# Gates of a top-2 expert layer carried in the scattered rows and applied where a tile's results leave PSUM

## The chip, the cores and the metric

The kernel runs on one NeuronCore of one Trainium2 chip. The metric is the device time of one launch in microseconds (us). TensorE (PE), VectorE (DVE), ScalarE (ACT), GpSimd (POOL) and SyncE (SP) each follow their own instruction stream; they meet only through semaphores. SP issues most DMAs, POOL the indirect ones that scatter rows.

## The reference, cut to what matters

Input `x` is 64 x 64 x 16 x 16 (f32). Two quantised 3x3 convolutions with batch norms form the first half, and a mixture of 8 experts with two choices for each of the 16384 tokens forms the second.

```python
x = x + conv_ref(ln_over_channels(x), ...)       # two BN + 4-bit act + 3x3 conv layers, plus residual
t = to_tokens(x)                                  # 16384 tokens x 64 channels
flat = layernorm(t)
logits = flat @ router_w.T                        # 8 experts
probs = softmax(logits)
topk_probs, topk_idx = top_k(probs, 2)
topk_probs = topk_probs / (sum(topk_probs, -1, keepdims=True) + 1e-09)
gates = einsum('nk,nke->ne', topk_probs, one_hot(topk_idx, 8))
h = silu(flat @ w1[e].T) * (flat @ w3[e].T)       # hidden size 682
y = h @ w2[e].T
t = t + einsum('ne,nec->nc', gates, y)            # only the two chosen experts count
x = from_tokens(t)
```

## The kernel before, in words

**Stages.** The image data lies as 16 stripes of 512 pixels by two halves of 64 channels, and stripes are worked in 8 pairs. First come the channel norm and the first convolution (to about 96 us of the span). Then follows the *route* stage (about 96 to 209 us): for each pair of stripes `route(p)` on each engine does the second convolution, the token norm, the router's logits, the choice of two experts and the slot of each token in a table of rows by expert, `expert_rows` in DRAM. A row holds 64 channels, the token's number and the preference code of its first choice (`ROW = C + 2`, line 43). Beside it the weights of one expert per pair are turned and written to DRAM (`stack_weights` on PE, line 1302, `w_stacked` copies on ACT, lines 685 to 690). Then a map of tiles is made on DVE (to about 218 us).

**Route on DVE** (line 950) is a chain of small instructions, each waiting for the one before. Work of the next pair is put between them: `add_conv` (line 942) for pair p+1, which needs that pair's convolution from PE, and the rounding of pair p+2. After `chosen` (line 994) PE makes the positions (lines 1323 to 1326) and the logits of pair p+1, and then the convolution of pair p+2 (line 1273). DVE takes the positions up at line 1002 and ends the pair with the slots (line 1008). The logits less their maximum stay in `lg` for all pairs, and the second choice's in `top2`.

**Route on ACT** (line 673) takes a square root of 16 numbers per row (line 675), two scaled copies for the rounding (649), four copies of the turned weights (685 to 690), two copies of the new x (668) and two squares (671). Exp of all pairs runs once after the last pair (lines 701 and 702), then Silu's table is fetched (703).

**Tiles.** 68 tiles of 512 rows (the last 12 are made of two halves with different experts) run through `tile` on every engine. SP loads rows and weights; PE turns the rows (1360), multiplies up (1387, both halves of the array), and down (1402), and turns the results back (1368); ACT does Silu (709 to 713) and the PSUM copies (720, 727); DVE multiplies (`hidden`, 1126 and 1130), copies the turned results to rows (`rows_out`, 1142) and prepares the tile after next (`split`, 1111 to 1117: which choice a row is, its target row, and a rearranged copy). POOL scatters 128 rows per instruction, in an order fixed when the program is built (lines 567 to 573): 256 scatters of token rows (551) and 270 of result rows (561). Result rows go to `result_rows` in DRAM, first choices in the lower half, second choices in the upper.

**Final stage.** When all scatters have landed, SP loads the results back as 8 pairs for each choice (486), named `y_and_rows` (first choice) and `conv_all` (second). For each pair ACT multiplies the first choice by its gate in 16 pieces (748), POOL the second choice in one instruction (581), DVE adds the two (1190), PE turns the sum (1430), DVE adds it to x (1185), and SP stores (494). SP issues no store before it has issued all loads. The gates themselves are computed on DVE from the exponentials (lines 1172 to 1178) while the last scatters run.

## Time and profile before

| what | value |
|---|---|
| median of 3 runs | 852.25 us (847.7 to 852.38) |
| profiled execution | 846.57 us, span 844.6 us, mean TensorE clock 0.929 |
| PE / PEld busy | 749.0 (89%) / 430.8 us (51%) |
| DVE / ACT / POOL busy | 553.6 (66%) / 491.9 (58%) / 557.2 us (66%) |
| route, 99 to 209 us | eight pairs, 11.3 to 14.7 us each |
| tiles, 226 to 792 us | 68 tiles, 8.26 us each |
| final stage, 800 to 844.6 us | loads, gates, sums, stores |

The span is cut into busy time by engine on the page; the idle time before an instruction and what ended it stand in brackets in a timeline. PE's clock is given as the share of full speed: 1.00 is 2.4 GHz and 0.50 is 1.2 GHz. POOL's busy time leaves out the 0.30 us between two of its scatters, so 66% does not mean a third of it is free.

### The profile page before, as it was taken

The page shows a single profiled execution, that of the slowest core. Times are in us where ns is not written, and L with a number is a line of the kernel's source. Part 1 is how long each engine was busy: PE and PEld are TensorE (multiplying, and loading weights), DVE is VectorE, ACT ScalarE, POOL GpSimd, SP SyncE. Part 2 cuts the span into 40 slices and gives each one's busy share as a digit, 9 for nine tenths or more (in the row PEclk, how much of TensorE's full clock was granted, in tenths as well). Part 3 has the DMA queues.
Part 4 walks back from the last instruction along what each step waited for, and adds up shares of the span by engine and source line. Part 5 has one row for each costly group of instructions (what it writes and reads, how often), then busy time and mean ns, then how long its engine had stood idle before and what let it go on. Part 6 is the DMA issues. An engine that isn't in the chain of part 4 may idle for free.

```text
span 844.6 us, 17550 instructions
## 1 busy us (share of the span) xinstructions
PE 749.0 (89%) x4875; PEld 430.8 (51%) x4875; DVE 553.6 (66%) x1326; ACT 491.9 (58%) x1127; POOL 557.2 (66%) x572
## 2 busy tenths in 40 slices
PE   5959688985499999999999999999999999999534
PEld 3734266664154555545454554545454557777323
DVE  5977578788466565666666565666676666666455
ACT  5836444333266666666666666666666566666285
POOL 3520027777777777777777777777777777777561
PEclk9959889897599999999999999999999999999855
DMA  8760023343344434343343434343334356656096
GB/s 199 133 111 0 0 62 102 112 135 108 103 120 122 127 108 126 110 117 113 112 113 112 121 104 127 114 112 113 112 113 111 113 158 180 191 168 181 26 387 195
DMA packets 84226, 104.98 MB, mean 124 GB/s; under 512 B 27061, under 2 KB 57966, under 8 KB 84176
## 3 DMA queue, kind: packets, MB, share of 16 engines
q1 hardware_dynamic: 65040, 83.17, 34.8%
q0 software_dynamic: 19136, 21.28, 9.3%
q14 instruction: 35, 0.29, 0.1%
q8 instruction: 15, 0.25, 0.1%
HBM read 73.62 MB, written 27.02 MB: 119 GB/s over the span
## 4 chain that ended last, share of the span: by engine, by line
PE 79%; DVE 9%; ACT 5%; issue 4%; DMA 1%; POOL 1%; DVEq 0%; SPq 0%; ACTq 0%; POOLq 0%
PE bank L1387 40%; PE bank L1402 21%; PE bank L1273 7%; ACT y_and_rows L748 4%; PE bank L1368 3%; PE bank L1360 2%; PE bank L1213 2%; PE bank L1218 1%; PE bank L1287 1%; PE bank L1294 1%; PE bank L1229 1%; DVE stats L972 1%; DMA conv_all<-result_rows 1%; DVE y_and_rows L959 0%; DMA w<-expert_w 0%
## 5 line engine op out<-in xcount | busy, mean ns | idle before, releaser
L551 POOL DMA_INDIRECT expert_rows<-y_and_rows,slot_all x256 | 249.4, 974 | 143.8 <-issue 77.2
L1126 DVE TENSOR_TENSOR conv_all<-conv_all,bank 128x512 f32<-128x512 f32 x340 | 233.7, 687 | 165.1 <-ACT conv_all L709 163.6
L1387 PE MATMUL bank<-xT,w 64*128 64x512 f32 (+1 forms) x1608 | 326.4, 536 | 1.8 <-DMA w<-expert_w 1.7
L709 ACT ACTIVATE conv_all<-bank 128x512 f32<-128x512 f32 x340 | 203.0, 597 | 118.3 <-PE bank L1387 118.0
L1387 PEld LDWEIGHTS bank<-xT,w 64*128 64x128 f32 x1608 | 144.9, 187 | 172.1 <-DVE conv_all L1126 85.4
L561 POOL DMA_INDIRECT result_rows<-conv_all,dest_all x142 | 140.1, 986 | 46.7 <-issue 41.8
L1402 PE MATMUL bank<-conv_all,w 128*64 128x256 f32 x1240 | 161.7, 384 | 1.2 <-DVE tile_map L1098 1.2
L1402 PEld LDWEIGHTS bank<-conv_all,w 128*64 128x64 f32 x1240 | 91.1, 136 | 51.6 <-issue 12.6
L720 ACT ACTIVATE xT<-bank 64x256 f32<-64x256 f32 x272 | 102.8, 378 | 14.1 <-PE bank L1360 11.7
L1273 PE MATMUL bank<-quant_padded,conv_w_blocks 128*128 128x512 bf16 x288 | 73.8, 418 | 8.7 <-issue 4.4
L727 ACT ACTIVATE conv_all<-bank 128x256 f32<-128x256 f32 x68 | 26.0, 383 | 86.0 <-PE bank L1402 86.0
L561 POOL DMA_INDIRECT result_rows<-result_rows,dest_all x64 | 63.2, 987 | 19.5 <-issue 19.2
L561 POOL DMA_INDIRECT result_rows<-squares,dest_all x64 | 63.0, 985 | 19.5 <-issue 19.2
L1273 PEld LDWEIGHTS bank<-quant_padded,conv_w_blocks 128*128 128x128 bf16 x288 | 29.7, 106 | 49.2 <-issue 15.4
L1130 DVE TENSOR_TENSOR rstd_wide<-conv_all,bank 42x256 f32<-42x256 f32 x136 | 52.0, 422 | 2.1
L1430 PE MATMUL bank<-ident,y_and_rows 128*128 128x128 f32 x64 | 15.7, 427 | 30.9 <-DVE y_and_rows L1190 30.9
L1402 PE MATMUL bank<-rstd_wide,w 128*64 128x256 f32 x248 | 40.9, 379 | 0.0
L748 ACT ACTIVATE y_and_rows<-y_and_rows,gates 128x64 f32<-128x64 f32 x128 | 30.7, 337 | 13.2 <-DMA conv_all<-result_rows 13.2
L1360 PE MATMUL bank<-ident,conv_all 128*128 128x128 f32 x136 | 26.3, 276 | 5.1 <-DVE conv_all L1117 5.1
L1368 PE MATMUL bank<-ident,conv_all 128*128 128x128 f32 x136 | 29.8, 301 | 0.5 <-ACT conv_all L727 0.5
L1430 PEld LDWEIGHTS bank<-ident,y_and_rows 128*128 128x128 f32 x64 | 12.6, 224 | 34.0 <-DVE y_and_rows L1190 34.0
L530 POOL DMA_DIRECT2D x_all<-y_and_rows x16 | 15.9, 1173 | 20.4 <-DVE y_and_rows L849 20.4
(248 smaller groups left out, 844.7 us busy)
## 6 DMA issues: line engine op xcount, KB each, us to landing
w<-expert_w SPq DMA_DIRECT2D x68, 384.0 KB
w<-expert_w SPq DMA_DIRECT2D x68, 192.0 KB
conv_all<-expert_rows SPq DMA_DIRECT2D x56, 132.0 KB
x_all<-in_x SPq DMA_DIRECT2D x16, 256.0 KB, 4.1
x_all<-y_and_rows POOLq DMA_DIRECT2D x16, 256.0 KB, 4.8
expert_rows<-y_and_rows,slot_all POOLq DMA_INDIRECT x256
y_and_rows<-result_rows SPq DMA_DIRECT2D x8, 512.0 KB, 9.8
conv_all<-result_rows SPq DMA_DIRECT2D x8, 512.0 KB, 10.6
```

The source lines that it names most:

```text
L551: nc.gpsimd.indirect_dma_start(xs, bass.IndirectOffsetOnAxis(ap=slot_all[:, s, k * GH + g:k * GH + g + 1], axis=0), rows_all[:, s, g, :], ...
L561: nc.gpsimd.indirect_dma_start(yout, bass.IndirectOffsetOnAxis(ap=dest_all[:, j, g:g + 1], axis=0), yrow[j % RING][:, g, :], None, bounds_ ...
L709: nc.scalar.activation(sbuf[k % 3], h1_ps[k % 3][:], ACT.Silu).then_inc(silu_rdy, 1)
L720: ins = nc.scalar.activation(xT[u][C * h:C * h + C, TH * t:TH * t + TH], turn_ps[C * t:C * t + C, 0:TH], ACT.Copy)
L748: ins = nc.scalar.activation(y[:, g, :], y[:, g, :], ACT.Copy, scale=gate[:, 0, 2 * p + g // GH, g % GH:g % GH + 1])
L1126: V.tensor_tensor(hbuf[k], sbuf[k % 3], h3_ps[k % 3][:], ALU.mult).then_inc(mul_rdy, 1)
L1130: ins = V.tensor_tensor(hbuf[k][0:HR, rows_], sbuf[k % 3][0:HR, rows_], ps[k % 3][TAIL3:TAIL3 + HR, rows_], ALU.mult)
L1273: ins = mm(conv_ps[u][:], wblk[:, l, t, :], qpad[u][:, :, ky:ky + H, kx:kx + W], start=t == 0, stop=t == TAPS - 1)
L1360: ins = nc.tensor.transpose(turn_ps[:, 128 * q:128 * q + 128], pairs_x[u][:, q, :], ident[:])
L1368: ins = nc.tensor.transpose(turn_ps[:, TH + 128 * q:TH + 128 * q + 128], ysb[u][:, 128 * q:128 * q + 128], ident[:])
L1387: ins = mm(ps[k % 3][:, rows_], w[half, cols], xT[u][half, rows_], start=True, stop=True)
L1402: ins = mm(y_ps[C * e:C * e + C, 0:TH], w2buf[e * two][u][:, i, :], hbuf[i][:, TH * e:TH * e + TH], start=i == 0, stop=i == KT - 1)
```

## The change

The row gets two more numbers (`ROW = C + 4`): the gate of the first choice, and what must be added to it to get the gate of the second. They are computed in every pair of the route stage, by `gates` on DVE (five instructions) from exponentials that ACT now makes pair by pair (`exps`). Sqrt and Exp lie in different activation tables, so ACT switches the table twice in each pair, each time by a dummy activation placed ahead (`load_table`). In a tile, `split` picks the gate of each row (two more instructions of 4 numbers each), and `rows_out` multiplies by it instead of copying. The final stage has only the sum on DVE; the multiplications on ACT (128 instructions) and on POOL (8) and the seven gate instructions on DVE are gone.

```diff
-    ROW = C + 2
+    ROW = C + 4
@@ POOL, end
-            pool.wait_ge(gate_rdy, 1)
-            for p in range(NP):
-                pool.wait_ge(yk_in[p], 32)
-                y = yk[1][p].rearrange("p (g c) -> p g c", g=GP)
-                nc.gpsimd.tensor_tensor(y, y, gate_of(1, p), ALU.mult).then_inc(g2_rdy, 1)
@@ ACT, route
+            def load_table(f):
+                k = (ACT.Sqrt, ACT.Exp, ACT.Silu).index(f)
+                nc.scalar.activation(table_first[:, k:k + 1], half_col[:, 0:1], f)
+            def exps(p):
+                act.wait_ge(ex_go, p + 1)
+                nc.scalar.activation(lg[:], lg[:], ACT.Exp)
+                nc.scalar.activation(top2[:], top2[:], ACT.Exp).then_inc(ex_rdy, 1)
             def route(p, first=False, last=0):
                 act.wait_ge(rsd_rdy, 2 * p + 1)
                 nc.scalar.activation(st[:, 1, :], st[:, 0, :], ACT.Sqrt).then_inc(rsd_rdy, 1)
+                load_table(ACT.Exp)
...
+                if first:
+                    exps(p)
+                if last != 1:
+                    keep_x1(p + 1)
+                if not first:
+                    exps(p)
                 if last != 1:
                     squares(p + 1)
+                    load_table(ACT.Sqrt)
@@ ACT, end
-            act.wait_ge(gate_rdy, 1)
-            for p in range(NP):
-                act.wait_ge(yk_in[p], 32)
-                y = yk[0][p].rearrange("p (g c) -> p g c", g=GP)
-                for g in range(GP):
-                    ins = nc.scalar.activation(y[:, g, :], y[:, g, :], ACT.Copy,
-                                               scale=gate[:, 0, 2 * p + g // GH, g % GH:g % GH + 1])
-                ins.then_inc(g0_rdy, 1)
@@ DVE, route
+            def gates(p, c, rows_p):
+                total, below = gsum[:, 0], gsum[:, 1]
+                first_gate, change = rows_p[:, :, C + 2], rows_p[:, :, C + 3]
+                dve.wait_ge(ex_rdy, p + 1)
+                c(V.tensor_reduce(total, lg[:], AX.X, ALU.add))
+                c(V.scalar_tensor_tensor(below, total, 1e-9, top2[:], ALU.mult, ALU.add))
+                c(V.tensor_scalar(below, below, 1.0, None, ALU.add))
+                c(V.reciprocal(first_gate, below))
+                V.scalar_tensor_tensor(change, top2[:], -1.0, first_gate, ALU.add, ALU.mult)
...
+                gates(p, c, rows_p)
                 dve.wait_ge(pos_rdy, p + 1)
@@ DVE, split
                     ins = V.tensor_scalar(second[u][:, n * i:n * i + n], xrow[u][:, n * i:n * i + n, C + 1],
-                                          expert_of[:, two, at], float(TOK), ALU.not_equal, ALU.mult)
+                                          expert_of[:, two, at], None, ALU.not_equal)
                 c(ins)
-                V.tensor_tensor(dest_all[:, j, :], second[u][:], xrow[u][:, :, C], ALU.add)
+                c(V.tensor_tensor(gate_change[u], second[u], xrow[u][:, :, C + 3], ALU.mult),
+                  lambda: V.scalar_tensor_tensor(dest_all[:, j, :], second[u], float(TOK), xrow[u][:, :, C],
+                                                 ALU.mult, ALU.add))
+                V.tensor_tensor(gate_of_row[j % 4], gate_change[u], xrow[u][:, :, C + 2], ALU.add)
@@ DVE, rows_out
-                V.tensor_copy(yrow[r].rearrange("p (t q) c -> p q t c", t=2),
-                              turn_ps[:, TH:T].rearrange("p (q t c) -> p q t c", q=2, t=2)).then_inc(yr_sb, 1)
+                V.tensor_tensor(yrow[r].rearrange("p (t q) c -> p q t c", t=2),
+                                turn_ps[:, TH:T].rearrange("p (q t c) -> p q t c", q=2, t=2),
+                                gate_of_row[v].rearrange("p (t q) -> p q t", t=2).unsqueeze(3)
+                                .broadcast_to([128, 2, 2, C]), ALU.mult).then_inc(yr_sb, 1)
@@ DVE, end
-            dve.wait_ge(ex_rdy, 2)
-            one(V.tensor_reduce(gsum[:], lg[:], AX.X, ALU.add))
...
             for p in range(NP):
-                dve.wait_ge(g2_rdy, p + 1)
-                dve.wait_ge(g0_rdy, p + 1)
+                dve.wait_ge(yk_in[p], 32)
                 V.tensor_tensor(yk[0][p], yk[0][p], yk[1][p], ALU.add).then_inc(g1_rdy, 1)
```

How the instructions move, at three places. First VectorE in the last pair of the route stage, from `chosen` to the slots, before (the pairs of the loop have the same order with the two rounding instructions of line 911 behind the first row):

```order
L994 TENSOR_TENSOR chosen<-one_hot 128x128
L1002 TENSOR_TENSOR positions<-bank,base 128x136
L1004 TENSOR_TENSOR route_slots<-one_hot,positions 128x256
L1005 COPY base<-positions 128x8
L1006 COPY base_by_stripe<-positions 128x16
```

and in the changed kernel, where `gate_sum` is `gsum` and `y_and_rows` the token rows:

```order
L998 TENSOR_TENSOR chosen<-one_hot 128x128
L948 TENSOR_REDUCE gate_sum<-logits 128x16
L949 SCALAR_TENSOR_TENSOR gate_sum<-gate_sum,second_minus_first 128x16
L950 TENSOR_SCALAR gate_sum<-gate_sum 128x16
L951 RECIPROCAL y_and_rows<-gate_sum 128x16
L952 SCALAR_TENSOR_TENSOR y_and_rows<-second_minus_first,y_and_rows 128x16
L1007 TENSOR_TENSOR positions<-bank,base 128x136
L1009 TENSOR_TENSOR route_slots<-one_hot,positions 128x256
```

Five instructions now stand between `chosen` and the positions. Second, ScalarE from the last weight copy of the seventh pair (the one behind the loop) into the eighth, before:

```order
L690 ACTIVATE w_stacked<-bank 42x64
L668 ACTIVATE x_all<-x_0 128x512
L668 ACTIVATE x_all<-x_1 128x512
L671 ACTIVATE squares<-bank 128x512 x2
L675 ACTIVATE stats<-stats 128x16
```

and now:

```order
L690 ACTIVATE w_stacked<-bank 42x64
L660 ACTIVATE x_all<-x_0 128x512
L660 ACTIVATE x_all<-x_1 128x512
L669 ACTIVATE logits<-logits 128x128
L670 ACTIVATE second_minus_first<-second_minus_first 128x16
L665 ACTIVATE squares<-bank 128x512 x2
L654 ACT_TABLE_LOAD
L654 ACTIVATE table_first<-half_col 128x1
L674 ACTIVATE stats<-stats 128x16
L654 ACT_TABLE_LOAD
L654 ACTIVATE table_first<-half_col 128x1
```

The two exponentials stand ahead of the squares, one table load behind the squares and one behind the square root. Third, VectorE at the end of one of the last tiles, before:

```order
L1142 COPY squares<-bank 128x2x2x64
L1111 TENSOR_SCALAR conv_all<-conv_all,tile_expert 128x2 x2
L1114 TENSOR_TENSOR dest_all<-conv_all 128x4
L1117 COPY conv_all<-conv_all 128x256
L1126 TENSOR_TENSOR conv_all<-conv_all,bank 128x512 x5
```

and now:

```order
L1149 TENSOR_TENSOR conv_all<-bank,conv_all 128x2x2x64
L1115 TENSOR_SCALAR conv_all<-conv_all,tile_expert 128x2 x2
L1118 TENSOR_TENSOR conv_all<-conv_all 128x4
L1119 SCALAR_TENSOR_TENSOR dest_all<-conv_all 128x4
L1121 TENSOR_TENSOR conv_all<-conv_all 128x4
L1124 COPY conv_all<-conv_all 128x256
L1133 TENSOR_TENSOR conv_all<-conv_all,bank 128x512 x5
```

Two small instructions come in, and the copy of the results has become a product with the gate.

## Rows read from the trace of the kernel before

**Rows 1.** The page: chain that ended last, by engine.

```profile
PE 79%; DVE 9%; ACT 5%; issue 4%; DMA 1%; POOL 1%; DVEq 0%; SPq 0%; ACTq 0%; POOLq 0%
```

**Rows 2.** Windows: start:end, length, busy us (instructions) of each engine, clock, DMA share, GB/s.

```profile
226.00:607.00 381.00, 381.00 (x2388) 192.24 (x2389) 240.97 (x520) 243.88 (x551) 290.43 (x298) 0.99 0.41 117
692.00:792.00 100.00, 99.52 (x867) 73.40 (x863) 63.35 (x140) 62.67 (x141) 73.69 (x76) 1.00 0.56 163
```

**Rows 3.** Timeline, DVE, end of a tile: start, us, instruction, [idle before <-releaser].

```profile
408.24 0.42 DVE L1142 COPY conv_all<-bank 128x256 f32<-128x256 f32 x1 [0.50 <-ACT xT L720]
408.83 0.21 DVE L1114 TENSOR_TENSOR dest_all<-conv_all 128x4 int32<-128x4 f32 x1
411.08 0.69 DVE L1126 TENSOR_TENSOR conv_all<-conv_all,bank 128x512 f32<-128x512 f32 x1 [1.83 <-ACT conv_all L709]
```

**Rows 4.** Timeline, DVE, the sixth pair of the route stage.

```profile
177.55 0.25 DVE L825 RECIPROCAL stats<-stats 128x16 f32<-128x16 f32 x1 [0.28 <-ACT stats L675]
177.84 0.18 DVE L826 SCALAR_TENSOR_TENSOR stats<-stats 128x16 f32<-128x16 f32 x1
180.93 0.69 DVE L942 SCALAR_TENSOR_TENSOR x<-bank,x_all 128x512 f32<-128x512 f32 x1 [0.16 <-issue]
183.19 0.28 DVE L988 TENSOR_REDUCE second_minus_first<-route_a 128x128 f32 x1
186.16 0.30 DVE L1002 TENSOR_TENSOR positions<-bank,base 128x136 f32<-128x136 f32 x1 [0.19 <-PE bank L1326]
```

**Rows 5.** Timeline, DVE, its longer waits in other pairs of the route stage.

```profile
128.90 0.69 DVE L942 SCALAR_TENSOR_TENSOR x<-bank,x_all 128x512 f32<-128x512 f32 x1 [1.22 <-PE bank L1273]
130.93 0.69 DVE L942 SCALAR_TENSOR_TENSOR x<-bank,x_all 128x512 f32<-128x512 f32 x1 [1.14 <-PE bank L1273]
157.25 0.69 DVE L942 SCALAR_TENSOR_TENSOR x<-bank,x_all 128x512 f32<-128x512 f32 x1 [1.46 <-PE bank L1273]
197.47 0.30 DVE L1002 TENSOR_TENSOR positions<-bank,base 128x136 f32<-128x136 f32 x1 [0.87 <-issue]
207.98 0.30 DVE L1002 TENSOR_TENSOR positions<-bank,base 128x136 f32<-128x136 f32 x1 [1.32 <-issue]
```

**Rows 6.** Timeline, PE: the convolution of a pair at either clock.

```profile
150.61 6.34 PE L1273 MATMUL bank<-quant_padded,conv_w_blocks 128*128 128x512 bf16 x18
163.31 4.21 PE L1273 MATMUL bank<-quant_padded,conv_w_blocks 128*128 128x512 bf16 x18
```

**Rows 7.** Windows inside those two convolutions (columns as in Rows 2).

```profile
150.00:155.00 5.00, 5.00 (x15) 2.19 (x16) 4.28 (x14) 1.71 (x3) 3.78 (x5) 0.50 0.09 27
163.50:167.50 4.00, 4.00 (x20) 1.82 (x19) 3.35 (x10) 1.71 (x3) 3.01 (x4) 1.00 0.54 194
```

**Rows 8.** Timeline, ACT: the second pair, the sixth pair, and the two late table loads.

```profile
124.22 0.22 ACT L675 ACTIVATE stats<-stats 128x16 f32<-128x16 f32 x1 [1.50 <-DVE stats L973]
...
181.82 0.87 ACT L685 ACTIVATE w_stacked<-bank 128x512 f32<-128x512 f32 x2 [2.81 <-PE bank L1310]
184.90 1.10 ACT L671 ACTIVATE squares<-bank 128x512 f32<-128x512 f32 x2
...
210.83 1.28 ACT L703 ACT_TABLE_LOAD   x1
212.12 0.20 ACT L703 ACTIVATE silu_first<-half_col 128x1 f32<-128x1 f32 x1
```

**Rows 9.** Timeline, final stage: the three multiplying and adding engines.

```profile
805.08 30.66 ACT L748 ACTIVATE y_and_rows<-y_and_rows,gates 128x64 f32<-128x64 f32 x128 [13.16 <-DMA conv_all<-result_rows]
...
825.02 2.35 POOL L581 TENSOR_TENSOR conv_all<-conv_all,gates 128x1024 f32<-128x1024 f32 x1 [1.12 <-DMA conv_all<-result_rows]
...
835.84 1.23 DVE L1190 TENSOR_TENSOR y_and_rows<-y_and_rows,conv_all 128x1024 f32<-128x1024 f32 x1 [1.40 <-ACT y_and_rows L748]
```

**Rows 10.** Windows of the final stage (columns as in Rows 2).

```profile
802.00:825.00 23.00, 7.87 (x32) 6.28 (x32) 11.63 (x11) 19.92 (x84) 14.23 (x7) 0.50 1.04 386
839.50:844.10 4.60, 0.00 (x0) 0.00 (x0) 0.32 (x1) 0.00 (x0) 0.00 (x0) 0.50 0.83 228
```

More of the change, by code:

```diff
@@ L147, in conv_moe_kernel @@
         counts = bases[:, SNAPS[0] - 1:NS, :]
-        gate = sb("gates", [128, 2, NS, GH])
-        gsum = sb("gate_sum", [128, NS, GH])
         tm = sb("tile_map_work", [128, 8, LV, E])
@@ L192, in conv_moe_kernel @@
         second = [carve(4) for u in range(2)]
+        gate_change = [carve(4) for u in range(2)]
+        gate_of_row = [carve(4) for v in range(4)]
         ysb = [carve(TH) for u in range(2)]
@@ L359, in conv_moe_kernel @@
         fin_ps = [bank[0:2], bank[2:4]]
-        def gate_of(k, p):
-            return gate[:, k, 2 * p:2 * p + 2, :].rearrange("p a g -> p (a g)").unsqueeze(2).broadcast_to([128, GP, C])
         NSMALL = 2 + 1 + 1
@@ L668, in squares @@
                     nc.scalar.activation(stripe(xb, s), x1[u][:], ACT.Copy).then_inc(x1_kept, 1)
+            def squares(p):
                 for u in range(2):
@@ L691, in route @@
                                      ACT.Copy).then_inc(wt_sb, 1)
+                if first:
[4 more added lines that the diff above has]
+                    exps(p)
                 if last != 1:
                     squares(p + 1)
+                    load_table(ACT.Sqrt)
             for s in range(4):
                 affine(1, s, s % 2)
+            keep_x1(0)
             squares(0)
             pairs(act, route)
-            act.wait_ge(ex_go, 1)
-            nc.scalar.activation(lg[:], lg[:], ACT.Exp).then_inc(ex_rdy, 1)
-            nc.scalar.activation(top2[:], top2[:], ACT.Exp).then_inc(ex_rdy, 1)
-            nc.scalar.activation(silu_first[:], half_col[:, 0:1], ACT.Silu)
+            load_table(ACT.Silu)
             def silu(j, k):
@@ L1167, in _ @@
             rows_out(NT - 1, 3, (NT - 1) % RING)
-            g0, g1 = gate[:, 0], gate[:, 1]
-            dve.wait_ge(ex_rdy, 2)
-            one(V.tensor_reduce(gsum[:], lg[:], AX.X, ALU.add))
-            one(V.reciprocal(g0, gsum[:]))
-            one(V.tensor_tensor(g1, top2[:], g0, ALU.mult))
-            one(V.scalar_tensor_tensor(gsum[:], g0, 1e-9, g1, ALU.add, ALU.add))
-            one(V.reciprocal(gsum[:], gsum[:]))
-            for k in range(2):
-                ins = V.tensor_tensor(gate[:, k], gate[:, k], gsum[:], ALU.mult)
-            ins.then_inc(gate_rdy, 1)
             def add(p):
```

21 lines of the change are left out of this document (9 added, 12 removed).

## The prediction

> **What bounds the kernel now.** I read the chain of waits by engine first: PE holds 79% of it [rows 1]. Then the stages in windows. In the tile stage PE is busy 381.0 of 381 us and 99.5 of 100 [rows 2]; 68 tiles at 8.26 us. POOL has nearly no air either: 298 instructions with 0.30 us behind each are 290.4 + 89.4 = 379.8 us of 381, and in the second window 73.7 + 76 x 0.30 = 96.5 of 100 [rows 2]. DVE and ACT have a third of their time free there. Then a timeline of one tile: DVE ends its work behind a tile and waits 1.83 us for ACT's Silu of the next [rows 3]. In the route stage DVE is the bound of the pairs in which PE's clock is full: in the sixth pair the only waits over 0.2 us are for the square root, and DVE comes to `add_conv` with the convolution done, 0.16 us of issue [rows 4]. Where the clock is at half, DVE waits for the convolution, 1.22 and 1.14 us in the second pair and 1.46 in the fourth [rows 5]. Last the final stage: ACT's 128 multiplications run without a break for 30.66 us, while POOL, with 2.35 us per pair, waits for each load; the last pair's load is in by 825.02, its sum starts only at 835.84 [rows 9]. So ACT sets the end there, 10.8 us behind the data.
>
> **Final stage: a gain.** Removed: 128 ACT and 8 POOL instructions. The next limits are three.
> - The chain behind the last load. From the start of the last sum to the end of the span are 844.6 - 835.84 = 8.76 us [rows 9]. With the sum starting at 825.02 the end is 833.8, a gain of 10.8.
> - DVE itself: a sum of 1.23 us [rows 9] and two additions of 0.69 us (an addition from PSUM of this shape costs that, like 0.69 in [rows 4]) are 2.6 us per pair. Eight loads come between 805.1 and 825.0 [rows 9], 2.8 us apart. DVE just keeps up.
> - The DMA engines. They are full (share 1.04) at 386 GB/s from 802 to 825 [rows 10], 23 x 386 = 8.88 MB. The loads are 16 of 512 KB, 8.39 MB; so 0.49 MB of the 4.19 MB of stores is out by 825, and 3.70 MB are left. The stores no longer trickle behind ACT, they stand in a queue, so their rate decides. Upper end: 386 GB/s, 9.6 us, end 834.6. Lower end: the last four stores of before ran alone at 228 GB/s [rows 10]: 16.2 us, end 841.2. That row had a share of 0.83, so with a full queue it is 228 / 0.83 = 275 GB/s. As some stores will be mixed with loads I take 300: 12.3 us, 837.3. To that 0.5 us for the last landing (DMA is active to 844.1 in [rows 10], the span ends at 844.6).
>
> So the final stage ends near 837.8: **6.8 us gained**, between 2.9 and 9.5. The gate arithmetic that goes from DVE there ran beside the last scatters and is worth nothing.
>
> **Route stage: a loss on DVE.** `gates` adds a reduction of 128 numbers (0.28), three small instructions of 16 (0.18 each) and a reciprocal (0.25) [rows 4]. That is 1.07 us, with about 0.03 us of semaphore between each 1.2 us a pair. What covers it, pair by pair:
> - First pair: nothing, the next `add_conv` comes behind it in order. 1.2.
> - Second: the third pair has no wait for the convolution. 1.2.
> - Third: the fourth waits 1.46 us for its convolution [rows 5]. 0.
> - Fourth, fifth, sixth: only the 0.19 us wait for the positions [rows 4]. 3 x 1.0.
> - Seventh: 0.87 us before the positions [rows 5]. 0.3.
> - Eighth: 1.32 us before the positions, PE at half clock [rows 5]. 0.
>
> The waits of the second pair cover nothing, since its convolution is itself behind the first pair's delay. Sum **5.7 us**. If the waits covered all but the first two, 2.4; if none did, 9.6.
>
> **Route stage: ACT.** Per pair two table loads of 1.28 us with dummies of 0.20 [rows 8], and two exponentials of 128 and 16 numbers at 0.2 to 0.3 (the small activations of [rows 8] take 0.20 and 0.22): together 3.5 us. There is room: after the square root ACT waits 2.81 us for the weights, of which load and dummy take 1.5 [rows 8]. Tightest behind the squares is the second pair, with 1.50 us of idle before its square root [rows 8] against 1.48. The exponentials come behind the copies of x: in the sixth pair those end where the squares began, 184.90 [rows 8], so the exponentials end at 185.5, and DVE asks for them at 186.0, just before the old start of line 1002 [rows 4]. 0.5 us of margin. I cost ACT at nothing; if the cover goes, each late microsecond is one on DVE.
>
> The row shows that a table load costs its 1.28 us and no more: the next activation starts 0.01 us behind it [rows 8]. The Trainium skill (ScalarE: Activation LUTs, What ACT_TABLE_LOAD costs, and Table sets) puts a switch at 1283 ns and a drain of about 1380 ns more, and says to do all activations of one set before the next, which is just what this change gives up. By its 2.66 us, as an estimate, 14 more switches are 37 us of ACT; the second pair's square root would come some 1.4 us late and the rest would stay within the waits, so the sum would be about 1.5 us higher. The trace has the 1283 and not the drain.
>
> **Tile stage.** `split` gains two instructions of 4 numbers, 0.21 each [rows 3]. `rows_out` reads PSUM and multiplies instead of copying 256 columns, 0.42 [rows 3]; a product of twice the columns is 0.69 [rows 3], so the product lies between 0.42 and 0.69. At most 0.7 us more against 1.83 idle: hidden, in all tiles but two: the first, where the split is on the way to the first matmul (0.3), and the one in which DVE also places the half tiles, where its idle time is already used up (0.4). **0.7 us.**
>
> **POOL and the queues.** Token rows grow from 264 to 272 bytes. POOL's time is per instruction; if it went with the bytes instead, 3% of 256 x 0.97 is 7.5 us, and POOL has 3.5 us free in [rows 2] plus the later start of the tiles, 5.7 - 1.2 = 4.5, in which it runs ahead. So even then it is barely not the bound. I cost it at 0.
>
> **Sum.** 5.7 + 0.7 - 6.8 = -0.4: from 846.57 to 846.2 us. The profiled execution lay 5.7 us below the median of the runs shown and within them, so in their terms **852.0 us** (852.25 - 0.4, rounded).
>
> **The rivals.**
> - *The gain comes through and the route's loss does not* (13%). Half clock strikes the convolution in a few pairs, 6.34 us against 4.21 [rows 6], at clock 0.50 against 1.00 [rows 7]. PE works the same in a longer pair; should the drops fall elsewhere, in waits, the stage loses 1.5 instead of 5.7. With the final stage at the limit of its chain: 1.5 + 0.7 - 10.8 = -8.6, 843.7 against 852.25. For it: only three pairs are struck now. Against it: DVE's five instructions have no cover.
> - *PE's clock takes the route stage* (13%, slower). DVE's longer pair leaves PE waiting longer, and PE may drop to half clock in every pair. A convolution at half throughout is 2 x 4.21 = 8.4 us. In the fourth pair 6.34 us gave a wait of 1.46 [rows 5, 6]; with 8.4, and DVE 1.2 later, the wait is 1.46 + 2.1 - 1.2 = 2.4, in each of five pairs, 12 us, on top of the gates. It decides once a convolution passes 6.1 us. 852.0 + 12 = 864.
> - *ACT comes late* (4%, slower). If exponentials miss their 0.5 us margin, or Sqrt waits for its table, both loads of each pair enter DVE's chain: 8 x 1.3 to 8 x 2.6, 862 at the least. Against it: the idle times above.
> - *The product in `rows_out` or the wait for the gates delays the tiles*: needs 1.8 us per tile, which no row near it has (1%).
> - *DMA stores at 228 GB/s*: within my own case, +3.9.
>
> My forecast has 69%. **Range**: down, the final stage at 9.5 and a route of 2.4 (-6.4) and the lower runs of the same kernel (847.7, 4.5 below the median), partly together: 843. Up, 9.6 of route and 2.9 of gain (+7.4), and a part of the clock case: 861. A measurement here can tell about 1% from no change. Faster by over 1% (below 843.7) 0.13; within 0.69; slower 0.18.
>
> **What would show it.** Sums at line 1187 starting about 2.8 us apart, right behind the loads, the last near 825 plus the shift; DMA full between 802 and 838. In the route stage, pairs one, two, four, five and six 1 to 1.2 us longer, the third not; the start of the first tile at 226 + 6. Sixteen table loads of 1.28 us there, and no wait of line 948 for ACT. Tiles at 8.26 us as before. I am wrong if the convolution rows show half clock in more than three pairs, if the stores alone run nearer 228 or 386 GB/s, or if a DVE wait for ACT appears at line 948.

## The result, and the profile after

The changed kernel takes 846.36 us (median of 20 runs) against 849.91 us (20 runs of the kernel before on the same chip). The ratio is 0.9959, with a 95% interval of 0.9941 to 0.9978; in a later set of runs, on a chip of its own, the same kernel gave 0.9961 [0.9931, 0.9991]. So it is faster by 0.4%, within the 1% called no change above. The profiled execution went from 846.57 us (span 844.6) to 845.35 us (span 843.3, mean TensorE clock 0.925): -1.2 us where -0.4 was forecast. One further run of the changed kernel took 3324 us, once in 32, with no profile of it; the ratio leaves it out, and I have no cause for it.

By stages of the two profiled executions, each from the first instruction of its kind to that of the next stage:

| stage | before, us | after, us | measured | predicted |
|---|---|---|---|---|
| norm and first convolution, to the first rounding on DVE | 100.23 | 101.06 | +0.83 | 0 |
| route, to the map of tiles | 116.38 | 121.98 | +5.60 | +5.7 |
| map to first tile | 9.11 | 9.22 | +0.11 | 0 |
| tiles and last scatters | 574.42 | 575.40 | +0.98 | +0.7 |
| final, from the first load's issue | 44.46 | 35.64 | -8.82 | -6.8 |
| sum | 844.60 | 843.30 | -1.30 | -0.4 |

The chain of waits by engine answers to [rows 1]: ACT's share has fallen from 5% to 2%, DVE's has risen from 9% to 12%.

```profile
PE 75%; DVE 12%; issue 5%; DMA 2%; ACT 2%; SPq 2%; POOL 1%; DVEq 1%; POOLq 0%; ACTq 0%
```

The windows of the changed kernel, columns as in [rows 2]. The first two lie in the tile stage, moved by the 6 to 8 us by which it starts later; the others in the final stage and answer to [rows 10].

```profile
232.00:613.00 381.00, 380.74 (x2376) 191.84 (x2378) 249.86 (x608) 243.44 (x551) 290.00 (x297) 0.99 0.41 117
700.00:800.00 100.00, 99.44 (x864) 73.35 (x864) 64.76 (x158) 62.68 (x141) 70.69 (x72) 1.00 0.55 162
810.00:830.00 20.00, 11.81 (x48) 9.41 (x48) 14.35 (x17) 0.00 (x0) 0.00 (x0) 0.50 1.05 390
830.00:834.00 4.00, 3.04 (x13) 2.64 (x14) 3.75 (x6) 0.00 (x0) 0.00 (x0) 0.50 1.08 383
834.00:838.00 4.00, 0.90 (x5) 0.50 (x3) 1.45 (x3) 0.00 (x0) 0.00 (x0) 0.50 1.09 383
838.00:842.00 4.00, 0.00 (x0) 0.00 (x0) 0.00 (x0) 0.00 (x0) 0.00 (x0) 0.50 1.04 357
```

PE is as full in the tile stage as before. In the final stage the DMA engines are full from 810 us to the last store: the stores that ran with nothing beside them moved 383 and then 357 GB/s, not the 300 of the forecast. That rate is one of the prediction's own signs of being wrong ("nearer 228 or 386 GB/s"). The timeline of DVE there:

```profile
812.72 1.23 DVE L1187 TENSOR_TENSOR y_and_rows<-y_and_rows,conv_all 128x1024 f32<-128x1024 f32 x1 [12.33 <-DMA conv_all<-result_rows]
815.43 1.23 DVE L1187 TENSOR_TENSOR y_and_rows<-y_and_rows,conv_all 128x1024 f32<-128x1024 f32 x1 [1.49 <-DMA conv_all<-result_rows]
816.57 1.28 DVE L1183 TENSOR_TENSOR x_all<-x_all,bank 128x512 f32<-128x512 f32 x2
...
831.65 1.22 DVE L1187 TENSOR_TENSOR y_and_rows<-y_and_rows,conv_all 128x1024 f32<-128x1024 f32 x1 [0.26 <-DMA conv_all<-result_rows]
```

Eight sums, 2.71 us apart, each released by its load; the last starts at 831.65, 11.6 us before the end, where in [rows 9] it started 8.8 us before it. What follows the last sum is longer now (stores still queue), but it starts with the data.

The route stage. First VectorE in the fifth pair, from `chosen` to the next pair's reduction:

```profile
176.14 0.29 DVE L998 TENSOR_TENSOR chosen<-one_hot 128x128 bf16<-128x128 f32 x1
176.34 0.76 DVE L905 TENSOR_SCALAR quant_padded<-quant_tmp 128x512 bf16<-128x512 f32 x2
177.01 0.28 DVE L948 TENSOR_REDUCE gate_sum<-logits 128x16 f32<-128x128 f32 x1
177.33 0.17 DVE L949 SCALAR_TENSOR_TENSOR gate_sum<-gate_sum,second_minus_first 128x16 f32<-128x16 f32 x1
177.53 0.25 DVE L950 TENSOR_SCALAR gate_sum<-gate_sum 128x16 f32<-128x16 f32 x1
177.92 0.26 DVE L951 RECIPROCAL y_and_rows<-gate_sum 128x16 f32 x1
178.32 0.19 DVE L952 SCALAR_TENSOR_TENSOR y_and_rows<-second_minus_first,y_and_rows 128x16 f32 x1
178.43 0.29 DVE L1007 TENSOR_TENSOR positions<-bank,base 128x136 f32<-128x136 f32 x1
...
180.33 1.22 DVE L976 TENSOR_REDUCE stats<-squares 128x16 f32<-128x1024 f32 x1 [0.33 <-issue]
```

From the first of the five gate instructions (177.01) to the positions (178.43) are 1.42 us, with no wait for ACT and none for the matmuls of the positions, for which DVE waited 0.19 us before [rows 4]. In the fourth and the sixth pair (windows of 13.77 and 13.45 us) some instructions that stand in every pair take longer, here in the fourth the two roundings, 0.93 us where the fifth has 0.76:

```profile
162.70 0.93 DVE L905 TENSOR_SCALAR quant_padded<-quant_tmp 128x512 bf16<-128x512 f32 x2
```

Next PE and DVE in the second pair:

```profile
121.80 3.76 PE L1284 MATMUL bank<-centre_half,x 128*128 128x128 f32 x16 [3.72 <-DVE x L936]
126.22 1.22 DVE L976 TENSOR_REDUCE stats<-squares 128x16 f32<-128x1024 f32 x1 [2.63 <-ACT squares L665]
127.17 4.21 PE L1270 MATMUL bank<-quant_padded,conv_w_blocks 128*128 128x512 bf16 x18
```

The convolution, 5.46 us at this place in the kernel before and 6.34 us two pairs later [rows 6], now takes 4.21 us, here and in all seven that follow the first one (in the second profile of the changed kernel, `changed_again`, one of the seven took 5.69). Half clock has moved: it lies on PE's work behind its wait for `x`, where 16 small matmuls take 3.76 us (2.05 us at full clock, in a profile below). DVE waited for the squares before too, 1.35 us; now it is 2.63, and the two waits for the convolution [rows 5] are gone. The line of before:

```profile
122.76 1.22 DVE L972 TENSOR_REDUCE stats<-squares 128x16 f32<-128x1024 f32 x1 [1.35 <-ACT squares L671]
```

ScalarE in the fifth and sixth pair answers to [rows 8]:

```profile
175.25 0.31 ACT L669 ACTIVATE logits<-logits 128x128 f32<-128x128 f32 x1 [0.60 <-DVE token_no L994]
175.46 0.20 ACT L670 ACTIVATE second_minus_first<-second_minus_first 128x16 f32<-128x16 f32 x1
175.57 0.58 ACT L665 ACTIVATE squares<-bank 128x512 f32<-128x512 f32 x1
176.43 0.60 ACT L665 ACTIVATE squares<-bank 128x512 f32<-128x512 f32 x1 [0.28 <-PE bank L1284]
177.04 1.28 ACT L654 ACT_TABLE_LOAD   x1
178.34 0.20 ACT L654 ACTIVATE table_first<-half_col 128x1 f32<-128x1 f32 x1
181.84 0.22 ACT L674 ACTIVATE stats<-stats 128x16 f32<-128x16 f32 x1 [3.30 <-DVE stats L977]
182.07 1.28 ACT L654 ACT_TABLE_LOAD   x1
```

It waits for DVE ahead of the exponentials and, with the new table in place, 3.30 us for the square root's input. And one tile on DVE, answering to [rows 3]:

```profile
407.21 0.42 DVE L1149 TENSOR_TENSOR conv_all<-bank,conv_all 128x256 f32<-128x256 f32 x1 [0.49 <-ACT xT L724]
408.01 0.17 DVE L1118 TENSOR_TENSOR conv_all<-conv_all 128x4 f32<-128x4 f32 x1
410.05 0.69 DVE L1133 TENSOR_TENSOR conv_all<-conv_all,bank 128x512 f32<-128x512 f32 x1 [1.44 <-ACT conv_all L713]
```

The product costs the same 0.42 us as the copy; 1.44 us of the 1.83 us of idle are left.

### The profile page after: what moved, and what is told of

It reads as the page before. It is cut to its first block, busy times and chain, and to the rows that moved or that the text cites. A ratio compares the mean times of both kernels' runs of the same rounds, so it can differ in the third digit from the quotient of the medians.

```text
span 843.3 us, 17635 instructions
## 1 busy us (share of the span) xinstructions
PE 754.9 (90%) x4875; PEld 438.7 (52%) x4875; DVE 568.3 (67%) x1494; ACT 483.7 (57%) x1042; POOL 541.0 (64%) x564
## 4 chain that ended last, share of the span: by engine, by line
PE 75%; DVE 12%; issue 5%; DMA 2%; ACT 2%; SPq 2%; POOL 1%; DVEq 1%; POOLq 0%; ACTq 0%
PE bank L1384 40%; PE bank L1399 21%; PE bank L1270 5%; PE bank L1365 3%; PE bank L1357 2%; PE bank L1210 2%; DMA conv_all<-result_rows 1%; SPq L481 1%; PE bank L1215 1%; DVE stats L976 1%; PE bank L1226 1%; PE bank L1284 1%; DVE y_and_rows L963 1%; DMA w<-expert_w 0%; DVE stats L820 0%
## 5 line engine op out<-in xcount | busy, mean ns | idle before, releaser
L1270 PE MATMUL bank<-quant_padded,conv_w_blocks 128*128 128x512 bf16 x288 | 69.2, 399 | 8.7 <-issue 4.4
L1399 PE MATMUL bank<-conv_all,y_and_rows 128*64 128x256 f32 x120 | 28.5, 384 | 0.0
L1284 PE MATMUL bank<-centre_half,x 128*128 128x128 f32 x128 | 24.2, 366 | 4.5 <-DVE x L936 4.5
```

What stands on the lines that cost most here:

```text
L1270: ins = mm(conv_ps[u][:], wblk[:, l, t, :], qpad[u][:, :, ky:ky + H, kx:kx + W], start=t == 0, stop=t == TAPS - 1)
L1284: ins = mm(rT_ps[u][:, 128 * g:128 * g + 128], x1[u][:, 128 * g:128 * g + 128], centre[:], start=True, stop=True)
L1399: ins = mm(y_ps[C * e:C * e + C, 0:TH], w2buf[e * two][u][:, i, :], hbuf[i][:, TH * e:TH * e + TH], start=i == 0, stop=i == KT - 1)
```

## The experiments

Each ratio is to the kernel before on the same chip. Kernels marked "of before" are edits of the kernel before, the others of the changed one. For stages I read the profiles; one profile is one execution, so the end of this section says how far such readings differ.

**The final stage alone (of before).** The products go and nothing takes their place.

```diff
-                nc.gpsimd.tensor_tensor(y, y, gate_of(1, p), ALU.mult).then_inc(g2_rdy, 1)
...
-                for g in range(GP):
-                    ins = nc.scalar.activation(y[:, g, :], y[:, g, :], ACT.Copy,
...
-                dve.wait_ge(g2_rdy, p + 1)
-                dve.wait_ge(g0_rdy, p + 1)
+                dve.wait_ge(yk_in[p], 32)
```

> The kernel before, without the multiplications of the final stage (ACT's 128 and POOL's 8): the results are summed without their gates; route and tile stages are as before. My theory after the result: the final stage of the changed kernel, from the first load issued to the end, is 8.8 us shorter than before (35.6 against 44.5) because only the DMA engines limit it, at 386 GB/s for stores too. Then this kernel is 8.8 us faster than before (ratio 0.9896) and that stage takes 35.6 us. Rival, my prediction's term: stores alone run at 300 GB/s, 6.8 us (ratio 0.992).

Measured: 838.5 us, 0.9891 [0.9845, 0.9937]. The final stage takes 35.06 us, 9.4 less than 44.46, and its windows show the full queue to the end:

```profile
802.00:822.00 20.00, 13.78 (x56) 10.98 (x56) 16.59 (x20) 0.00 (x0) 0.00 (x0) 0.50 1.05 388
826.00:830.00 4.00, 0.00 (x0) 0.00 (x0) 0.00 (x0) 0.00 (x0) 0.00 (x0) 0.50 1.09 383
```

The second window holds stores only. So the gain belongs to the final stage, it is 9 us and not 7, and behind it the DMA engines are the limit: they are full to the end, and each sum but the first two waits only 0.2 to 0.3 us for its load.

**The rest of the change without the route's part.** No exponentials by pair, no table switches, no `gates`: the rows carry numbers that are not gates, everything behind them is as in the change.

```diff
-                load_table(ACT.Exp)
...
-                    load_table(ACT.Sqrt)
...
-                gates(p, c, rows_p)
```

> The changed kernel without the gates of the route stage: no exponentials, no table switches, none of the five DVE instructions; the two gate columns of a row hold what was there. Everything else of the change stays. Theory: the route stage gets back the 5.6 us between the fourth copy of the scaled input and the tile map, so the whole is 5.6 us under the changed kernel, 9 us under before (ratio 0.989). Rival: PE's clock falls at other places, and the stage gives back only 2 to 4 us or as much as 8.

Measured: 843.73 us, 0.9914 [0.9880, 0.9948]. Against the changed kernel's 0.9959 the gates give back 0.0045, 3.8 us; the intervals overlap. The profile's route stage is 118.10 us, 3.9 less than with gates (4.5 less than in the second profile of the changed kernel). That is not the 5.6 us of my theory; it is what the rival said, 2 to 4, for the reason that it gave. The rest of the change without the route's part is thus worth 0.0086, 7.3 us, of the 9.4 us of the final stage. In this profile PE's clock fell at another place: the third convolution took 6.88 us, and the second pair lasted 16.01 us.

```profile
131.90 6.88 PE L1263 MATMUL bank<-quant_padded,conv_w_blocks 128*128 128x512 bf16 x18
```

From the third pair to the sixth the pairs last 12.28, 12.23, 12.22 and 11.89 us; with gates 13.34, 13.77, 13.34 and 13.45. So the gates cost **1.1 us in two of them and 1.5 in the other two**, where 1.2 had been added up. The dearer pairs are the fourth and the sixth. In both the changed kernel takes 0.43 us more up to the slots than in the pair before, and it lies, all but one part, in instructions that stood there before: the two roundings at line 905 take 0.93 us for 0.76, one at line 900 0.50 for 0.42, line 977 0.21 for 0.17, and line 950 of the gates 0.37 for 0.25. What makes them longer stays open; taking the table loads away (next experiment) leaves the pattern as it is.

**The switches alone.** The table loads go and Exp becomes Copy (no switch, the gates are wrong numbers); and the other way, each load is doubled.

```diff
-                nc.scalar.activation(lg[:], lg[:], ACT.Exp)
+                nc.scalar.activation(lg[:], lg[:], ACT.Copy)
...
-                load_table(ACT.Exp)
```

```diff
+                load_table(ACT.Silu, 3)
                 load_table(ACT.Exp)
...
+                    load_table(ACT.Silu, 4)
                     load_table(ACT.Sqrt)
```

> The changed kernel with the table switches of the route stage taken away: the two Exp of each pair are plain copies and the 15 dummy activations with their loads in the pairs are gone; DVE's five gate instructions and all waits stay, the gates come out as other numbers. Theory: the 1.28 us loads lie in ACT's idle time, so this equals the changed kernel (ratio to before 0.996), but for the square root of the second pair, 0.03 us late there. Rival: ACT is on the path in the route stage (a switch costs more than its load, as the Trainium skill's page ScalarE: Activation LUTs, What ACT_TABLE_LOAD costs, has it with 2.66 us): 1.5 to 3 us come back (ratio 0.993).

> The changed kernel with two switches in place of each in the route stage (by way of Silu's table), 2 x 1.48 us more of ACT per pair. Theory from the trace of the changed kernel: the exponentials were done 0.7 to 1.35 us before DVE asked for them and waited 0.6 to 0.9 us for DVE themselves, so 1.48 us more is nearly covered in the middle pairs; the square root of the second pair comes 1.5 us late. Whole: 1.5 to 3 us slower than the changed kernel (ratio 0.998 to 1.000). Rival: ACT had no cover, every pair gets 2 to 3 us longer, 16 to 24 us in all.

Measured: 847.45 us, 0.9989 [0.9962, 1.0015] without, 847.62 us, 0.9992 [0.9961, 1.0023] doubled. Both ran on a chip where the kernel before had a median of 847.12 and not 849.91, which can be why the ratios stand higher than the changed kernel's 0.9959; the changed kernel itself was not run there. Between the two there is no difference that the intervals (0.3%, 2.5 us) can tell, nothing comes back without the loads, and the route stage without switches (121.78 us) is the one with them (121.98). The fifteen loads that were taken out cost nothing on the path. Doubled they show. The profiled execution of that kernel, the slowest of its 12 runs (852.93 us), has a route stage of 126.51 us, 3.9 and 4.5 more than in the two profiles with single switches. Of these about 1.8 are ACT's (0.40, and 1.69 for 0.28): DVE waits for the exponentials in the first pair and for the square root in the second, where the room was tightest.

```profile
131.60 1.28 ACT L654 ACT_TABLE_LOAD   x1
132.90 0.20 ACT L654 ACTIVATE table_first<-half_col 128x1 f32<-128x1 f32 x1
133.01 0.20 ACT L674 ACTIVATE stats<-stats 128x16 f32<-128x16 f32 x1
```

```profile
122.19 0.29 DVE L950 TENSOR_REDUCE gate_sum<-logits 128x16 f32<-128x128 f32 x1 [0.40 <-ACT second_minus_first L670]
133.24 0.25 DVE L821 RECIPROCAL stats<-stats 128x16 f32<-128x16 f32 x1 [1.69 <-ACT stats L674]
206.50 0.69 DVE L938 SCALAR_TENSOR_TENSOR x<-bank,x_all 128x512 f32<-128x512 f32 x1 [1.49 <-PE bank L1272]
```

DVE waits 1.69 us for a square root that takes 0.28 us to come elsewhere. Another 2.26 us lie in the seventh pair, where a convolution ran at half clock (6.37 us) and DVE waited 1.49 us for it; whether the doubled loads brought that about isn't shown. The median doesn't show any of it; the rival of 16 to 24 us is out.

**Wide rows alone (of before).**

```diff
-    ROW = C + 2
+    ROW = C + 4
```

> The kernel before with rows of 68 numbers in place of 66 and nothing else. Theory: POOL's time is per instruction, 0.97 us per scatter, and the loads of rows hide: same as before (ratio 1.000). Rival: scatters cost by bytes, 3% more each; POOL would have 1.00 us per scatter and the tiles' results come up to 3 us late at the end.

Measured: 847.0 us, 0.998 [0.9948, 1.0012]. The scatters of token rows, 974 ns each before, take 975:

```profile
L551 POOL DMA_INDIRECT expert_rows<-y_and_rows,slot_all x256 | 249.5, 975 | 144.1 <-issue 77.5
```

Between 264 and 272 bytes a row POOL's price is per instruction, not per byte.

**Gates in the tiles, two ways.** The row carries the second choice's logit less the first's (`ROW = C + 3`). In a tile the gate is a function of it: a first choice's is 1/2 (1 + tanh(-d/2)), a second's the same with d changed in sign, so one activation of 4 numbers per tile makes it, and no exponential is left. The 1/2 goes into the turned `w2`. The first version uses Tanh:

```diff
+                nc.scalar.activation(gate_of_row[v], gate_change[u], ACT.Tanh)
...
+                V.scalar_tensor_tensor(yrow[r], gate_of_row[v].unsqueeze(2).broadcast_to([128, 4, C]), 1.0,
+                                       turn_ps[:, TH:T].rearrange("p (g c) -> p g c", c=C),
+                                       ALU.add, ALU.mult).then_inc(yr_sb, 1)
```

the second Sigmoid with scale 2.0, and no 1/2.

> A version meant to keep the gain and drop the loss. The gate of two choices is 1/(1+exp(-d)) with d the difference of their logits, so the row carries d alone (DVE's reduction writes it straight into the row), and per tile ACT takes one Tanh of 4 numbers per partition; the product in rows_out becomes (t+1) x result, and half the second weights takes the factor 0.5. No exponentials, no switches, no gate instructions in the route stage. Theory: ratio 0.989 like the kernel without gates, tiles at 8.26 us. Rival: the Tanh between the copies of x and of the results delays ACT in each tile by 0.2 us, 68 x 0.2 = 14 us, and it ends slower than before.

> The version with the difference of the logits in the row, with Sigmoid in place of Tanh: Silu and Tanh share a table, Sigmoid does not, so ACT switches twice in every tile. Theory (a switch costs its 1.28 us load alone): ACT's work per tile goes from 5.3 + 0.2 to 8.1 us, a little under the 8.26 us of PE, and as the loads stand between PSUM copies that PE waits for, tiles get 0 to 1 us longer, ratio 0.99 to 1.07. Rival (a drain of 1.38 us with each load, the skill's same section): 10.8 us per tile, 173 us more in all, ratio 1.19.

Measured: Tanh 842.99 us, 0.9907 [0.9874, 0.9939], equal to the change without gates (0.9914) within the intervals. Sigmoid 906.65 us, 1.068 [1.0612, 1.0749]. ScalarE in a tile with Sigmoid:

```profile
405.93 1.28 ACT L721 ACT_TABLE_LOAD   x1
407.22 0.20 ACT L721 ACTIVATE conv_all<-conv_all 128x4 f32<-128x4 f32 x1
407.44 0.38 ACT L726 ACTIVATE conv_all<-bank 128x256 f32<-128x256 f32 x1
407.84 1.28 ACT L707 ACT_TABLE_LOAD   x1
409.13 1.58 ACT L707 ACTIVATE conv_all<-bank 128x512 f32<-128x512 f32 x3
...
415.12 1.28 ACT L721 ACT_TABLE_LOAD   x1
```

Silu and Tanh share a table, no load appears between them; Silu and Sigmoid do not. Two loads, 2.56 us, stretch a tile from 8.26 to 9.19 us (405.93 to 415.12): here idle time takes up 1.63 us of them and no more, and 68 tiles make 63 us. Behind each load the activation starts 0.01 us later. The Trainium skill (ScalarE: Activation LUTs, What ACT_TABLE_LOAD costs) has some 1380 ns of drain on top of the load; two of these would, as an estimate from the page, add 2.8 us to each tile. No run here shows them. Its advice to keep to one set (Table sets) holds in the tiles, for the load itself (0.9907 against 1.068); in the route stage two switches a pair cost nothing on the path, and with four a pair DVE waited some 1.8 us more in all.

**TensorE's clock kept.** PE gets matmuls that nobody reads, put where it would wait: 12 (18 in the changed kernel) in the first pair, 6 in each later pair before the positions.

```diff
+            def keep_clock(n):
+                for _ in range(n):
+                    mm(bank[4][:, 128:512], ones_bf[:], wblk[:, 1, 0:3, :].rearrange("p t c -> p (t c)"),
+                       start=True, stop=True)
...
+                    keep_clock(12)
...
+                    if not first:
+                        keep_clock(6)
```

> The kernel before with the unread matmuls on PE in the route stage (12 ahead of the second pair's rows, 6 in each later pair). Theory: PE's clock stays full there, pairs take 13.0, 12.5 and then 12.2 us, the route stage (from the first rounding to the tile map) takes 112 to 113 us against 116.4 in the profile of before: ratio 0.995. Rival: the clock of the stage costs nothing on the path and the ratio is 1.000.

> The changed kernel with the same matmuls (18 ahead of the second pair's rows, since PE waits longer there, then 6 a pair). Theory: what is left between this route stage and that of the kernel before with the same matmuls is the gates alone: 1.12 to 1.5 us in each of the first seven pairs, 0.3 in the seventh, 0 in the eighth, 7 to 8 us; the stage takes 119.5 to 120.5 us, and the whole is 1 to 2 us faster than the changed kernel. Rival: the gates cost 5.7 us as predicted and the stage takes 118.

> The changed kernel once more, beside the others on one chip. Expected: ratio to before 0.996, route stage 119 to 123 us by where PE's clock falls, final stage 35.6 us.

> The Tanh version with matmuls on PE that nobody reads, in places where PE waits in the route stage: 12 of 128x384 bf16 before the second pair's rows are turned, and 6 in each later pair before the positions. In the profiles taken so far a pair lasts 12.2 us where PE's clock stays at full, and 13.8 to 16.0 us where it falls to half after such a wait. Theory: the clock no longer falls, the first two pairs take 13.0 and 12.3 us in place of 14.7 and 16.0, and the whole is 4 to 5 us faster than the Tanh version (ratio 0.985 to 0.986). Rival: the extra matmuls themselves hold up the positions by up to 1 us a pair, and the clock falls all the same: 0 to 6 us slower than the Tanh version.

> The Tanh version with the unread matmuls once more, on the same chip. Expected: ratio to before 0.988, route stage 112.4 us.

Measured:

| kernel | median, us | ratio | 95% | route stage of its profile, us |
|---|---|---|---|---|
| before, clock kept | 847.61 | 0.997 | 0.9938 to 1.0002 | 112.23 |
| changed, clock kept | 842.92 | 0.9932 | 0.9897 to 0.9967 | 121.09 |
| changed, again | 844.8 | 0.9961 | 0.9931 to 0.9991 | 122.60 |
| Tanh, clock kept | 837.57 | 0.9879 | 0.9836 to 0.9922 | 112.43 |
| Tanh, clock kept, again | 835.95 | 0.9848 | 0.9805 to 0.9891 | 112.39 |

Windows of the route stage in the Tanh version with the clock kept, and the small matmuls and convolution of its second and third pair:

```profile
114.00:127.00 13.00, 11.94 (x93) 8.35 (x92) 11.20 (x35) 5.55 (x11) 5.17 (x5) 1.00 0.33 98
127.00:140.00 13.00, 12.44 (x96) 8.89 (x94) 11.07 (x38) 5.21 (x12) 9.90 (x11) 1.00 0.40 116
180.00:194.00 14.00, 12.88 (x113) 9.24 (x111) 12.00 (x41) 4.57 (x11) 10.65 (x12) 1.00 0.43 121
```

```profile
129.99 2.05 PE L1278 MATMUL bank<-centre_half,x 128*128 128x128 f32 x16
131.88 1.14 PE L1323 MATMUL bank<-conv_w_blocks,ones_bf 128*128 128x384 bf16 x6
...
135.26 4.21 PE L1264 MATMUL bank<-quant_padded,conv_w_blocks 128*128 128x512 bf16 x18
```

Both are from the second set, `tanh_clock_again`. The granted clock is 1.00 from 114 to 194 us, where the changed kernel's was 0.55 from 118.0 to 125.6 us, in and behind PE's longest wait, and 0.72 from 146 to 152. Six matmuls of 1.14 us a pair buy this, in time in which PE had nothing to do. In the changed kernel the trick is worth little by its profile (121.09 us against 121.98 and 122.60, where 119.5 to 120.5 had been expected), since there half clock had already left the convolutions, and two later ones took 5.68 and 5.81 us in spite of it. In the kernel before the ratio, 0.997, does not by itself tell the matmuls from no change; the profiles do, 116.38 us of route stage against 112.23 and 846.57 us of execution against 842.60.

With the clock mostly out of the way the price of the gates is plainer. The route stages differ by 121.09 - 112.23 = 8.9 us; 0.8 of it lies ahead of the first pair's reduction, where the first convolution took 6.27 us against 5.47. The seven windows between the reductions differ by 1.20, 1.47, 1.04, 1.55, 1.12, 1.55 and 0.18: **8.1 us**, against 5.5 in the same windows of the plain kernels. The 2.6 us between are what half clock had cost the kernel before (4.1 us in these windows) beyond what it costs the changed one (1.5).

The Tanh version with the clock kept computes the whole reference and beats both kernels: 1.2 to 1.5% faster than before, about 1% than the change. None of its 12 runs is above 841.3 us, and none of the 97 of the kernel before is below 843.8.

How far one profile's route stage carries. An execution has a short start or a long one: the first rounding comes at 100.1 to 101.2 us or at 103.9 to 104.9 us, whatever the kernel. Without gates and without kept clock the stage took 113.97, 116.38 and 116.64 us behind a short start and 118.01, 118.10 and 118.14 behind a long one. With gates it took 121.78 (no switches) and 121.98 behind a short start, 122.60 behind a long one. Most of the difference is in the first two pairs (12.98 + 12.23 us at best, 14.72 + 16.02 at worst), by where half clock falls. With the clock kept it is gone (112.23, 112.39, 112.43), but all three of these had a short start. Against profiles with a short start the matmuls give 1.5 to 4.4 us.

The runs of a kernel split into groups in the same way. Each profiled execution lies in the group that its start suggests; for the runs without a profile that isn't shown. With the clock kept the kernel before has 5 runs from 842.3 to 843.6 us (the profiled one, short start, is 842.60) and 7 from 847.5 to 849.4. The changed kernel has 6 from 842.1 to 843.0 and 3 from 847.1 to 847.6 (the profiled one, long start, is 847.64). Its better ratio, 0.9932 against 0.997, is thus for the most part a matter of how many runs fell into which group; group against group the two are within about 1 us. The Tanh version has 4 runs from 835.3 to 838.7 and 8 from 842.9 to 844.0, with the clock kept 9 from 834.8 to 838.6 and 3 from 840.6 to 841.3. By the groups' medians the matmuls give 1.3 and 2.1 us there; the rest of what the ratios show (2.4 us in the first set, less than the 4 to 5 expected, and 5 in the second) is the share of the groups. Of the 5.6 us by which the route stages of these profiles differ (118.01 and 112.43) some 2.3 were lost again behind it: tiles and last scatters took 574.31 us, then 575.67 and 575.16, the final stage 35.29, then 36.36 and 36.52.

## Why the prediction was right, point by point

**Final stage: the mechanism right, the size too small.** Forecast 6.8 us, measured 8.8. The sums came 2.7 us apart behind their loads. Two terms make the 2.0 us of error. From the issue of the first load to the last sum it took 23.99 us (807.66 to 831.65), where the prediction kept the 24.88 of before (800.14 to 825.02): 0.9 us. Behind that came 11.65 us where 12.3 + 0.5 had been forecast: 1.1 us. The mis-sized term there is the rate of the stores. I took 300 GB/s, near the lower end that I had worked out from a queue that was not full (275). From 831.65 to 842.8 the queue moved 350 GB/s, 3.90 MB and not 3.70, and the stores alone ran at 383, then 357. The share of 0.83 in [rows 10] was an average over a trickling queue; the row to go by was the one with a share above 1.0, though it was made mostly of loads.

**Route stage: the sum right by luck, its parts not.** By windows from one pair's reduction to the next:

| pair | 1 | 2 | 3 | 4 | 5 | 6 | 7 | 8 |
|---|---|---|---|---|---|---|---|---|
| predicted | 1.2 | 1.2 | 0 | 1.0 | 1.0 | 1.0 | 0.3 | 0 |
| measured | +2.46 | -1.10 | +1.04 | -0.02 | +1.11 | +1.55 | +0.45 | -0.06 |

(and +0.17 ahead of the first). The third and fourth come to 1.02 together where 1.0 was forecast: the wait of 1.46 us [rows 5], which stands in the fourth window, is gone, and one pair's gates with it. But the profile doesn't show that the gates covered it, since the convolution that it was for ran in 4.21 us and not 6.34. (Begun at 151.82 us, it would at 6.34 have ended at 158.16, just when DVE came for it, at 158.17; so by this estimate the wait would have gone either way.) The first two come to 1.36 instead of 2.4. The sentence that failed is "the waits of the second pair cover nothing": its convolution went back to full clock, so 1.22 and 1.14 us of waits [rows 5] went, and the wait for the squares in the window before grew by 1.28 us, from 1.35 to 2.63. Pairs 5 to 7 cost 3.1 instead of 2.3: I had counted 0.19 and 0.87 us of cover there, and less was had. The two errors nearly cancel, and that 5.6 us met 5.7 is luck: with the clock kept in both kernels the same five instructions cost 8.1 us in these windows, 1.0 to 1.55 in each of the first six, with next to no cover. What was left out of the sum is that the longer pair moves the places where PE's clock falls. The sign given beforehand (pairs one, two, four, five and six longer, the third not) did not come: pairs one, three, five and six are longer, the second is shorter.

**ACT at nothing: right.** The loads took 1.28 us; ACT stood ready 3.3 us ahead of the square root in the sixth pair and had no idle left in the second (126.20, the load; 127.50, the dummy; 127.68, the square root), with DVE's reciprocal at the usual 0.28 us behind. Line 948 never waited for the exponentials. Removing the loads changed nothing; doubling them brought waits of 0.40 and 1.69 us in the first two pairs, so the room was nearly used up.

**Tiles, POOL: right.** +0.98 us for 0.7, though the same stage took 573.61 us in the second profile of the changed kernel, less than before, so one pair of profiles doesn't resolve the term. A scatter takes 976 and 986 ns (974 and 986 before).

**The rivals.** "The gain and no loss" did not happen: half clock did fall elsewhere, as that rival asked, but the five instructions had no cover. "PE's clock takes the route stage" is refuted by the convolution rows at 4.21 us, seven of seven in one profile and six in the other: the longer pair left PE's clock in the convolutions better than before, not worse. ACT late and the product in `rows_out` did not come.

**The median fell further than the profiles, by 3.5 us to 1.2.** In 97 runs of the kernel before over four sets, 42 lie above 851 us; of 31 runs that the ratios of the changed kernel use, none is above 849.7. At the low end of one set the two kernels are nearly alike, 844.06 and 843.43. None of the runs above 851 of the kernel before was profiled, so their cause is argued and not shown. Its profiled execution had a short start (100.23 us) and a route stage of 116.38; a long start would add 4 us, and all three profiles without gates behind a long start have a route stage of about 118.1, 1.7 more. The estimate is 846.57 + 4 + 1.7 = 852.3, where the group lies. The changed kernel went with a long start to 848.17 (profiled). So the change looks worth some 4 us behind a long start and 1.2 behind a short one. The kernel before with its clock kept has no run above 849.5 in 12, which fits.

## What to carry to other kernels

Work that is taken off an engine at the end of a kernel is paid by the queue that then stands full, so read that queue's rate where its share is above 1.0; and work that is put into a chain of small dependent instructions on the engine that bounds a stage is paid in full, 1.1 to 1.5 us for five of them here. If the same value can be made later by an engine with idle time, in a table that it has loaded anyway (Tanh beside Silu), both costs go. Before costing an edit in a stage where TensorE has waits, ask what the clock does there, since it hid 2.6 us of 8.1 here. A few unread matmuls in the waits took 4.2 us from the stage and 4.0 from the execution in the profiles of the kernel before, and 1.3 to 2.1 us from the Tanh version's groups of runs. And when an early stage ends 4 us sooner or later from one execution to the next, compare profiles and runs of the same kind before a difference of a few us is put down to the edit.

## What was not expected of the hardware

- Stores alone moved 383 GB/s, as much as loads (390 GB/s with both), as long as the queue was full; with gaps it was 228 [rows 10].
- Silu and Tanh need no table load between them, Silu and Sigmoid two per change and back; a load takes 1.28 us, and the next activation starts 0.01 to 0.02 us behind it.
- Without the gates in the route stage, TensorE's clock stayed at 1.00 from 114 to 194 us with 6 unread matmuls, 1.14 us, in the waits, and the stage took the same time within 0.2 us in three profiles (112.23 to 112.43 us; 113.97 to 118.14 without them). With the gates two convolutions still fell to 5.68 and 5.81 us, at a granted clock of 0.72.
- The start of the program has two lengths, whatever the kernel: the first rounding came at 100.1 to 101.2 us in eight profiles and at 103.9 to 104.9 us in the other six. Between 60 and 80 us the granted clock was 0.89 to 0.93 in the former and 0.77 to 0.80 in the latter.
